# Layer-norm statistics of two tiles in one VectorE instruction, and x + beta divided between GpSimd and VectorE

## The chip, the cores and the metric

The kernel runs on one core of one Trainium2 chip. The metric is the device time of one execution in microseconds. Three runs of the kernel before gave 680.88, 681.93 and 682.16 us; the median is 681.93 us.

## The reference

One layer of a graph network with 50000 nodes of 128 features, 25000 edges sorted by their target, 32 features per edge and one number (coordination) per node, all in f32:

```python
h = maximum(layernorm(x), 0)                       # no gamma, beta
e = concat(h[src], h[dst], edge_attr, c[src], c[dst])
messages = silu(e @ mW1 + mb1) @ mW2 + mb2
aggregated = segment_sum(messages, dst)            # per node
u = silu(concat(h, aggregated, c) @ uW1 + ub1) @ uW2 + ub2
out = x + layernorm(h + u) * gamma + beta
```

So there are three layer norms: of the rows gathered for an edge's two ends, of each node's own row, and of the update h + u. Each needs the mean and the variance of 128 numbers per row.

## The kernel before, in words

Work goes in steps. An edge step takes 512 edges: 4 tiles of 128 edges for each of two ends, gathered from HBM by eight indirect DMAs which GpSimd issues (L452). A node step takes 1024 nodes, 8 tiles of 128 nodes. Both kinds have 49 steps. Iteration n of the pipeline works on edge step n and, four behind it (NODE_LAG), on node step n - 4, with further stages of neighbouring steps in the same iteration. Each engine runs its own program, and semaphores tie them. `PIPELINES` says which iterations stand in the hardware loop of four iterations (9 to 44 before); those ahead and behind are unrolled, and 54 is the last.

VectorE's iteration, in its order (function `body` from L858, `k` is the node step of the iteration, `prev` and `done` the two before it, `later` and `ahead` the node steps two and four further, `new` the edge step):

- `y_stat` and `finish` for each of 8 tiles in turn: statistics of the update of `prev` (L935, read from PSUM), and the output of `done`, centred * rstd + x_beta (L902);
- `sum_means` (L944, y_sum), then `match_nodes(0)` (L888, builds the 0/1 matrix by which TensorE sums messages into nodes), `halve_means` (L951, y_mean), `match_nodes(1)`;
- `centre` for 8 tiles (L872): (update - mean) * gamma, which frees the PSUM tile ps_upd for TensorE;
- statistics of the 8 gathered tiles of `new` (L986, L987), after their gathers have landed;
- the chain from statistics to rstd and -mean * rstd: s_sub, s_add, s_m2, s_sq, var, guess, root_a, root_e, root_p, root_q, root_r, rstd, minus (L1004 to L1039), on 24 columns, one per tile. The statistics of x for `ahead` (L925) stand between them as fillers. ScalarE normalises with the result.

A `bn_stats` instruction gives six numbers per partition: count, mean and sum of squared deviations of the elements at even places, and the same three for the odd places. On one tile of 128 features the two halves have to be joined, which is what y_sum, y_mean, s_sub, s_add, s_m2, s_sq and var do.

x + beta (x_beta) is read by `finish` two iterations after it is made. GpSimd makes it for a whole node step in one instruction (L475), after its eight gathers and after both matches of the iteration (`match_ready`); for the first two node steps VectorE does (L916). GpSimd also loads gamma, beta and iota rows (`load_rows`, L488 to L493), between the gathers of edge step 0 and those of step 1. x itself is loaded by ScalarE's queue (L672), the message windows by SyncE's, eight loads per step (L393), which must follow the storing of the messages (L367).

TensorE's iteration: first layer of the edges (L531, L532, L535), turning of coordinates and x_norm (L543, L553), second layer (L563, L565), node products with `match` (L605, L608), turning of ends_norm (L576), update (L620, L622).

Of the kernel before, what the change touches and what calls it, by code (L numbers as in the profile page):

```python
# [6 lines left out]
P = 128  # L7
H = 128
# [3 lines left out]
EPS = 1e-5  # L12
# [123 lines left out]
PIPELINES = {WHOLE: (9, 45, NODE_STEPS + NODE_LAG + 2),  # L136
# [16 lines left out]
def gnn_layer(nc, rows, x_steps, ends, dst_all, dst_seen, attr, node_vec, mW1, mb1, mW2, mb2, uW1, ub1, uW2, ub2,  # L153
# [17 lines left out]
    with ctx:  # L171
# [55 lines left out]
        stats = sb("stats", [P, NS, 6])  # L227
        s_add, s_sub, s_m2, s_sq, var = (sb(n, [P, NS]) for n in ("s_add", "s_sub", "s_m2", "s_sq", "var"))
        y_sum, y_mean = sb("y_sum", [P, N_TILES]), sb("y_mean", [P, N_TILES])
# [42 lines left out]
        x_beta_ready, x_norm_ready = sem("x_beta_ready"), sem("x_norm_ready")  # L272
# [4 lines left out]
        y_mean_ready, half_out = sem("y_mean_ready"), sem("half_out")  # L277
# [34 lines left out]
        def _(sp):  # L312
# [125 lines left out]
            sp.dma_start(msgs[EDGES_PAD:MSG_ROWS, :], zeros[:, 0:2, :].rearrange("p a b -> p (a b)")[:, 0:MSG_ROW]).then_inc(tail_cleared, 16)  # L438
            sp.wait_ge(first_ready, 1)
# [8 lines left out]
        def _(pool):  # L448
# [8 lines left out]
            def body(it):  # L457
# [30 lines left out]
            def load_rows():  # L488
                for dst, source in (
                        (gamma_row[:, 0, :], gamma.rearrange("(o n) -> o n", o=1).broadcast_to([P, H])),  # L490
                        (beta_row[:, 0, :], beta.rearrange("(o n) -> o n", o=1).broadcast_to([P, H]))):
                    pool.dma_start(dst, source).then_inc(late_loaded, 16)
                pool.dma_start(iota[:, :, :].rearrange("p j m -> p (j m)"), iota_row.rearrange("(o n) -> o n", o=1).broadcast_to([P, N_STEP])).then_inc(iota_loaded, 16)  # L493

            run_steps(pool, body, scatter, load_rows)
# [139 lines left out]
        def _(act):  # L635
# [25 lines left out]
            def body(it):  # L661
# [4 lines left out]
                def load_nodes():  # L666
# [4 lines left out]
                    act.wait_ge(x_beta_ready, further.n - RING + 1)  # L671
                    act.dma_start(x_in[further.slot][:, :, :], x_v[further.n]).then_inc(x_loaded[further.slot], 16)  # L672
# [116 lines left out]
        STAT_OPS = 10  # L789
# [6 lines left out]
        def _(dve):  # L796
# [61 lines left out]
            def body(it):  # L858
                new = it.edge(0)
                ahead, nxt, later, k, prev, done = it.node(4), it.node(3), it.node(2), it.node(0), it.node(-1), it.node(-2)  # L860
                b, was = it.phase % RING, (it.phase - 1) % RING

                def centre(j):
# [3 lines left out]
                    if j == 0:  # L867
                        dve.wait_ge(y_mean_ready, 2 * prev.n + 2)
# [3 lines left out]
                    last = V.scalar_tensor_tensor(centred[:, j, :], ps_upd[:, j * P:(j + 1) * P], y_mean[:, j:j + 1], gamma_row[:, 0, :],  # L872
# [20 lines left out]
                def finish(j):  # L893
# [3 lines left out]
                    if j == 0:  # L897
                        dve.wait_ge(centred_ready, 2 * done.n + 2)
                        dve.wait_ge(rstd_ready, 2 * it.stats_before())
                        dve.wait_ge(x_beta_ready, done.n + 1)  # L900
                        wait(dve, stored[done.half], 16 * done.fills2)
# [7 lines left out]
                def add_beta():  # L909

                    if not later or k:
                        return
                    wait(dve, out_ready, later.n - RING + 1)
                    if isinstance(later.n, int) and later.n == 0:
                        dve.wait_ge(late_loaded, 16 * N_LATE)
                    V.tensor_tensor(x_beta[later.slot][:, :, :], x_in[later.slot][:, :, :],  # L916
# [196 lines left out]
```

## Time and profile before

| | |
|---|---|
| median of three runs | 681.93 us |
| the profiled execution: time | 680.75 us |
| its span, first to last instruction | 678.9 us |
| granted TensorE clock, mean | 0.986 of full |
| TensorE busy | 623.9 us (92%) |
| VectorE busy | 618.1 us (91%) |
| ScalarE busy | 545.7 us (80%) |
| GpSimd busy | 496.5 us (73%), of it 382.4 in 392 gathers and 111.3 in 47 x_beta |
| largest waits | GpSimd's gathers, issue, 106.4; ScalarE's hidden_n for TensorE 57.1; VectorE for gathers 23.6; TensorE for match 16.7 |

GpSimd's issue gaps, some 0.3 us ahead of each gather, belong to issuing a gather, so its load is its busy time and these. Three engines are busy for nine tenths of the span or close to it once that is counted, so shares of busy time don't tell which one sets the pace; the rows of one step, in order of time, do. Instructions on VectorE overlap: one starts before the last has ended, so the distance between starts, not the duration, is what an instruction costs there.

### The profile page before, as it was taken

To read this page: it belongs to the slowest core of one execution; us is meant where nothing else is said; L and a number is where in the kernel's file an instruction comes from. 1 tells how busy PE (TensorE), PEld (TensorE's weight loads), DVE (VectorE), ACT (ScalarE), POOL (GpSimd) and SP (SyncE) were. 2 spreads that over 40 slices of the span, in tenths; PEclk is the share of its full clock that TensorE was granted. 3 is DMA by queue.
4 is the path that set the end of the run, shared out by engine and by line. 5 is a ranking of instruction groups with operands and counts; after the bars stand their busy time and mean duration, and the time that the engine had idled before them with its cause. 6 is when DMAs were issued, how large, how long until landed. Compare 5 with 4: busy or idle time off the path is not lost.

```text
span 678.9 us, 17136 instructions
## 1 busy us (share of the span) xinstructions
PE 623.9 (92%) x3764; PEld 449.7 (66%) x3764; DVE 618.1 (91%) x2905; ACT 545.7 (80%) x1181; POOL 496.5 (73%) x447
## 2 busy tenths in 40 slices
PE   2889999999999999999999999999999999999982
PEld 1346787676676676676676676676676676776662
DVE  4747999999999999999999999999999999999887
ACT  1468999888888888888888888888888888899720
POOL 7778887887787787887787887887787788874200
PEclk9988999999999999999999999999999999999987
DMA  4645476677677677577677577676677677674422
GB/s 109 219 119 136 138 215 195 166 206 194 164 199 199 164 199 199 166 201 195 164 207 191 164 202 195 165 200 197 164 200 198 162 198 202 179 218 119 130 80 98
DMA packets 91986, 119.05 MB, mean 175 GB/s; under 512 B 20250, under 2 KB 65493, under 8 KB 91944
## 3 DMA queue, kind: packets, MB, share of 16 engines
q1 hardware_dynamic: 64436, 43.37, 23.9%
q0 software_dynamic: 12752, 26.57, 20.3%
q10 hardware_dynamic: 14756, 48.66, 19.0%
q8 instruction: 13, 0.21, 0.1%
q14 instruction: 29, 0.24, 0.1%
HBM read 79.63 MB, written 38.70 MB: 174 GB/s over the span
## 4 chain that ended last, share of the span: by engine, by line
POOL 27%; DVE 27%; issue 24%; PE 9%; DMA 8%; ACT 2%; SPq 1%; DVEq 1%; POOLq 0%; ACTq 0%
POOL ends_in L452 27%; DVE y_out L902 7%; DMA ends_in<-in_rows,end_idx 6%; DVE stats L935 5%; DVE stats L925 3%; DVE centred L872 3%; DVE stats L987 2%; DVE stats L986 2%; SPq L393 1%; PE ps_hid L608 1%; PE ps_upd L620 1%; ACT ends_norm L682 1%; PE ps_t L576 1%; PE ps_e L565 1%; PE ps_hid L605 1%
## 5 line engine op out<-in xcount | busy, mean ns | idle before, releaser
L452 POOL DMA_INDIRECT ends_in<-in_rows,end_idx x392 | 382.4, 975 | 114.8 <-issue 106.4
L682 ACT ACTIVATE ends_norm<-ends_in,minus,rstd 128x128 f32<-128x128 f32 x392 | 160.3, 482 | 5.9 <-DVE minus L1039 5.5
L682 ACT ACTIVATE x_norm<-x_in,minus,rstd 128x128 f32<-128x128 f32 x392 | 155.5, 481 | 0.0
L608 PEld LDWEIGHTS ps_hid<-match,msg_in 113*128 113x128 f32 x784 | 99.6, 191 | 78.5 <-DVE match L888 48.8
L475 POOL TENSOR_TENSOR x_beta<-x_in,beta_row 128x1024 f32<-128x1024 f32 x47 | 111.3, 2367 | 30.7 <-DVE y_out L902 18.5
L902 DVE SCALAR_TENSOR_TENSOR y_out<-centred,rstd,x_beta 128x128 f32<-128x128 f32 x392 | 128.1, 336 | 2.7 <-issue 0.4
L608 PE MATMUL ps_hid<-match,msg_in 113*128 113x128 f32 x784 | 107.6, 280 | 17.5 <-DVE match L888 16.7
L935 DVE BATCH_NORM_STATS2 stats<-ps_upd 128x6 f32<-128x128 f32 x392 | 109.8, 289 | 4.5 <-issue 4.0
L780 ACT ACTIVATE hidden_n<-ps_hid,node_bias 128x512 f32<-128x512 f32 x98 | 67.0, 683 | 58.0 <-PE ps_hid L608 57.1
L620 PE MATMUL ps_upd<-w_out,hidden_n 128*128 128x128 f32 x784 | 104.7, 277 | 5.2 <-DVE centred L872 5.2
L872 DVE SCALAR_TENSOR_TENSOR centred<-ps_upd,y_mean,gamma_row 128x128 f32<-128x128 f32 x392 | 107.3, 338 | 0.0
L925 DVE BATCH_NORM_STATS2 stats<-x_in 128x6 f32<-128x128 f32 x392 | 100.7, 283 | 0.7
L605 PE MATMUL ps_hid<-h_t,w_node 128*128 128x512 f32 x196 | 100.7, 595 | 0.0
L620 PEld LDWEIGHTS ps_upd<-w_out,hidden_n 128*128 128x128 f32 x784 | 96.2, 193 | 5.8 <-DVE centred L872 5.8
L888 DVE SCALAR_TENSOR_TENSOR match<-iota_sb,const_sb,msg_in 112x512 f32<-112x512 f32 x98 | 73.2, 752 | 8.1 <-DMA msg_in<-msgs 6.7
L986 DVE BATCH_NORM_STATS2 stats<-ends_in 128x6 f32<-128x128 f32 x196 | 54.7, 279 | 24.3 <-DMA ends_in<-in_rows,end_idx 23.6
L706 ACT ACTIVATE h_t<-ps_t,b_col 128x1024 f32<-128x1024 f32 x49 | 54.5, 1113 | 16.1 <-PE ps_t L553 15.2
L742 ACT ACTIVATE ends_t<-ps_t 128x1024 f32<-128x1024 f32 x49 | 50.2, 1024 | 12.5 <-PE ps_t L576 12.5
L622 PE MATMUL ps_upd<-const_sb,h_t 128*128 128x128 f32 x392 | 59.4, 275 | 0.0
L576 PE MATMUL ps_t<-const_sb,ends_norm 128*128 128x128 f32 x392 | 51.9, 276 | 4.2 <-ACT ends_norm L682 4.2
L535 PE MATMUL ps_e<-feat_t,w_feat 34*128 34x512 f32 x98 | 55.0, 642 | 0.0
L987 DVE BATCH_NORM_STATS2 stats<-ends_in 128x6 f32<-128x128 f32 x196 | 54.0, 275 | 0.0
(92 smaller groups left out, 787.6 us busy)
## 6 DMA issues: line engine op xcount, KB each, us to landing
out<-y_out ACTq DMA_DIRECT2D x48, 512.0 KB, 2.9
x_in<-in_x_steps ACTq DMA_DIRECT2D x44, 512.0 KB
msg_in<-msgs SPq DMA_DIRECT2D x392, 56.4 KB
msgs<-msg SPq DMA_DIRECT2D x49, 258.0 KB, 2.5
ends_in<-in_rows,end_idx POOLq DMA_INDIRECT x392
feat_t<-in_attr SPq DMA_DIRECT2D x25, 128.0 KB
x_in<-in_x_steps SPq DMA_DIRECT2D x5, 512.0 KB
feat_t<-coords SPq DMA_DIRECT2D x98, 2.0 KB
```

The lines of the kernel that those rows point to most:

```text
L452: nc.gpsimd.indirect_dma_start(out=dst, out_offset=None, in_=rows, in_offset=bass.IndirectOffsetOnAxis(ap=end_idx[s.slot // 2][:, s.slot % ...
L475: nc.gpsimd.tensor_tensor(x_beta[later.slot][:, :, :], x_in[later.slot][:, :, :], beta_row[:, :, :].broadcast_to([P, N_TILES, H]), ALU.add ...
L605: nc.tensor.matmul(ps_hid[:, bank], w_node[:, :], h_t[k.half][:, bank], start=True, stop=False)
L608: last = nc.tensor.matmul(ps_hid[:, cols(j)], msg_in[k.half][0:WINDOW + 1, j, 0:H], match[k.half][0:WINDOW + 1, j, :], start=False, stop=j ...
L620: nc.tensor.matmul(ps_upd[:, cols(j)], hidden_n[:, cols(j)], w_out[:, :], start=j == tiles[0], stop=False)
L682: return nc.scalar.activation(dst, source, function, bias=minus[was][:, c:c + 1], scale=rstd[was][:, c:c + 1])
L872: last = V.scalar_tensor_tensor(centred[:, j, :], ps_upd[:, j * P:(j + 1) * P], y_mean[:, j:j + 1], gamma_row[:, 0, :], ALU.subtract, ALU. ...
L888: V.scalar_tensor_tensor(match[k.half][0:WINDOW, tiles, :], iota[0:WINDOW, tiles, :], const[0:WINDOW, bass.ds(C_BASE + N_TILES * k.n, 1)], ...
L902: last = V.scalar_tensor_tensor(y_out[done.half][:, j, :], centred[:, j, :], rstd[was][:, Y_AT + j:Y_AT + j + 1], x_beta[done.slot][:, j, ...
L925: last = V.bn_stats(stats[:, X_AT + j, :], x_in[n.slot][:, j, :])
L935: last = V.bn_stats(stats[:, Y_AT + j, :], ps_upd[:, j * P:(j + 1) * P])
L986: V.bn_stats(stats[:, t, :], ends_in[new.slot][:, 0, t, 0:H])
```

## The change

- `bn_stats` reads two neighbouring tiles at once, with the view `p t f -> p f t`: element 0 of the first tile, element 0 of the second, element 1 of the first, and so on. The even places are then the first tile and the odd ones the second, so the six numbers are count, mean and squared deviations of each. y_sum, y_mean, s_sub, s_add, s_m2 and s_sq go; `var` is one operation on the stored squares, `centre` and `minus` read the mean from the statistics. A step has 12 statistics instructions on 256 elements instead of 24 on 128. The fillers in the chain are four pairs. The statistics have two buffers now, since those of `ahead` are written while the iteration's own are read.
- x_beta: GpSimd makes the first four tiles of a node step (semaphore x_beta_head), VectorE the last four, at the end of its iteration behind `minus`. The first two node steps stay whole on VectorE.
- SyncE issues the loads of gamma, beta and iota, near its start, ahead of its wait for first_ready.
- The hardware loop covers iterations 11 to 46 instead of 9 to 44.

```diff
-PIPELINES = {WHOLE: (9, 45, NODE_STEPS + NODE_LAG + 2),
+PIPELINES = {WHOLE: (11, 47, NODE_STEPS + NODE_LAG + 2),
...
-        stats = sb("stats", [P, NS, 6])
+        stats = [sb(f"stats{b}", [P, NS, 3]) for b in range(2)]
...
+            for dst, source in (
+                    (gamma_row[:, 0, :], gamma.rearrange("(o n) -> o n", o=1).broadcast_to([P, H])),
+                    (beta_row[:, 0, :], beta.rearrange("(o n) -> o n", o=1).broadcast_to([P, H]))):
+                sp.dma_start(dst, source).then_inc(late_loaded, 16)
+            sp.dma_start(iota[:, :, :].rearrange("p j m -> p (j m)"), iota_row.rearrange("(o n) -> o n", o=1).broadcast_to([P, N_STEP])).then_inc(iota_loaded, 16)
             sp.wait_ge(first_ready, 1)
...
-                    if isinstance(later.n, int) and later.n == 2:
-                        pool.wait_ge(x_beta_ready, 2)
-                    else:
-                        wait(pool, match_ready, 2 * later.n - 2)
-                    nc.gpsimd.tensor_tensor(x_beta[later.slot][:, :, :], x_in[later.slot][:, :, :],
-                                            beta_row[:, :, :].broadcast_to([P, N_TILES, H]), ALU.add).then_inc(x_beta_ready, 1)
+                    wait(pool, match_ready, 2 * later.n - 2)
+                    nc.gpsimd.tensor_tensor(x_beta[later.slot][:, 0:N_TILES // 2, :], x_in[later.slot][:, 0:N_TILES // 2, :],
+                                            beta_row[:, :, :].broadcast_to([P, N_TILES // 2, H]), ALU.add).then_inc(x_beta_head, 1)
...
+                def pair_stats(into, c, tiles):
+
+                    return V.bn_stats(into[:, c:c + 2, :].rearrange("p c s -> p (c s)"), tiles.rearrange("p t f -> p f t"))
...
-                    if not later or k:
-                        return
+                    if not later:
+                        return
+                    if k:
+                        dve.wait_ge(x_loaded[later.slot], 16 * (later.fills4 + 1))
                     wait(dve, out_ready, later.n - RING + 1)
...
+                    tiles = slice(HALF if k else 0, N_TILES)
+                    V.tensor_tensor(x_beta[later.slot][:, tiles, :], x_in[later.slot][:, tiles, :],
+                                    beta_row[:, :, :].broadcast_to([P, tiles.stop - tiles.start, H]), ALU.add).then_inc(x_beta_ready, 1)
...
-                V.tensor_tensor(s_sub[:, at], stats[:, at, 1], stats[:, at, 4], ALU.subtract).then_inc(stat_ops, 1)
-                V.tensor_tensor(s_add[:, at], stats[:, at, 1], stats[:, at, 4], ALU.add)
                 if late:
-                    halve_means()
-                V.scalar_tensor_tensor(s_m2[:, at], stats[:, at, 2], H * EPS, stats[:, at, 5], ALU.add, ALU.add).then_inc(stat_ops, 1)
+                    dve.wait_ge(y_stats, prev.n + 1)
+                V.tensor_scalar(var[:, at], own_stats[:, at, SQUARES], 1.0 / H, EPS, ALU.mult, ALU.add).then_inc(stat_ops, 1)
+                between(0)
                 dve.wait_ge(stat_ops, base + 1)
-                V.scalar_tensor_tensor(s_sq[:, at], s_sub[:, at], 0.25, s_sub[:, at], ALU.mult, ALU.mult).then_inc(stat_ops, 1)
-                dve.wait_ge(stat_ops, base + 2)
-                between(0)
-                dve.wait_ge(stat_ops, base + 3)
-                V.scalar_tensor_tensor(var[:, at], s_m2[:, at], 1.0 / H, s_sq[:, at], ALU.mult, ALU.add).then_inc(stat_ops, 1)
-                between(1)
...
-                V.scalar_tensor_tensor(minus[b][:, at], s_add[:, at], -0.5, rstd[b][:, at], ALU.mult, ALU.mult).then_inc(rstd_ready, 1)
+                V.scalar_tensor_tensor(minus[b][:, at], own_stats[:, at, MEAN], -1.0, rstd[b][:, at], ALU.mult, ALU.mult).then_inc(rstd_ready, 1)
+                if k:
+                    add_beta()
```

## Rows read from the trace of the kernel before

**Rows 1.** Stretches, all engines: length, busy us (instructions) of each engine, clock, DMA.
```profile
65.84:113.85 48.01, 48.01 (x306) 36.06 (x305) 44.23 (x207) 44.24 (x98) 38.97 (x34) 1.00 0.63 186
...
267.00:369.00 102.00, 98.18 (x611) 71.42 (x610) 97.69 (x459) 88.88 (x194) 80.41 (x73) 1.00 0.68 187
...
572.73:622.25 49.52, 49.07 (x307) 35.73 (x305) 48.41 (x230) 44.36 (x98) 37.76 (x34) 1.00 0.66 193
...
634.25:678.90 44.65, 26.88 (x165) 21.02 (x163) 36.13 (x170) 12.33 (x23) 2.35 (x1) 0.86 0.28 92
```

**Rows 2.** Time order, TensorE, first edge product: start us, us, engine, line.
```profile
65.84 1.02 PE L531 MATMUL ps_e<-ends_t,w_src 128*128 128x512 f32 x2
...
113.85 1.02 PE L531 MATMUL ps_e<-ends_t,w_src 128*128 128x512 f32 x2
...
634.25 1.02 PE L531 MATMUL ps_e<-ends_t,w_src 128*128 128x512 f32 x2
```

**Rows 3.** Time order, VectorE, one step and the next one's end.
```profile
301.80 0.29 DVE L986 BATCH_NORM_STATS2 stats<-ends_in 128x6 f32<-128x128 f32 x1 [0.38 <-DMA ends_in<-in_rows,end_idx]
...
303.49 0.20 DVE L1004 TENSOR_TENSOR s_sub<-stats 128x24 f32<-128x24 f32 x1
...
306.51 0.18 DVE L1039 SCALAR_TENSOR_TENSOR minus<-s_add,rstd 128x24 f32<-128x24 f32 x1
...
310.51 0.16 DVE L944 TENSOR_TENSOR y_sum<-stats 128x8 f32<-128x8 f32 x1
310.71 0.80 DVE L888 SCALAR_TENSOR_TENSOR match<-iota_sb,const_sb,msg_in 112x512 f32<-112x512 f32 x1
311.43 0.29 DVE L951 TENSOR_SCALAR y_mean<-y_sum 128x8 f32<-128x8 f32 x1
311.51 0.74 DVE L888 SCALAR_TENSOR_TENSOR match<-iota_sb,const_sb,msg_in 112x512 f32<-112x512 f32 x1
...
314.24 0.28 DVE L986 BATCH_NORM_STATS2 stats<-ends_in 128x6 f32<-128x128 f32 x1
...
327.35 0.29 DVE L986 BATCH_NORM_STATS2 stats<-ends_in 128x6 f32<-128x128 f32 x1
```

**Rows 4.** Time order, GpSimd, the same step.
```profile
312.33 2.36 POOL L475 TENSOR_TENSOR x_beta<-x_in,beta_row 128x1024 f32<-128x1024 f32 x1 [0.59 <-DVE match L888]
...
314.84 0.96 POOL L452 DMA_INDIRECT ends_in<-in_rows,end_idx  x1 [0.16 <-issue]
...
323.76 0.95 POOL L452 DMA_INDIRECT ends_in<-in_rows,end_idx  x1 [0.30 <-DVE y_out L902]
```

**Rows 5.** Time order, VectorE, late node step: eight statistics without other work between.
```profile
651.13 1.67 DVE L935 BATCH_NORM_STATS2 stats<-ps_upd 128x6 f32<-128x128 f32 x8
```

**Rows 6.** Groups by shape, VectorE: busy us, mean ns, idle before.
```profile
L1004 DVE TENSOR_TENSOR s_sub<-stats 128x24 f32<-128x24 f32 x44 | 9.2, 209 | 1.5
...
L1010 DVE SCALAR_TENSOR_TENSOR s_sq<-s_sub 128x24 f32<-128x24 f32 x44 | 7.6, 174 | 0.0
...
L1004 DVE TENSOR_TENSOR s_sub<-stats 128x8 f32<-128x8 f32 x5 | 0.8, 166 | 0.0
...
L1010 DVE SCALAR_TENSOR_TENSOR s_sq<-s_sub 128x8 f32<-128x8 f32 x5 | 0.8, 159 | 0.0
```

**Rows 7.** The whole x + beta on VectorE (groups, time order), a gather beside it.
```profile
L916 DVE TENSOR_TENSOR x_beta<-x_in,beta_row 128x1024 f32<-128x1024 f32 x2 | 2.4, 1218 | 0.0
...
41.85 1.22 DVE L916 TENSOR_TENSOR x_beta<-x_in,beta_row 128x1024 f32<-128x1024 f32 x1
...
42.47 1.42 POOL L452 DMA_INDIRECT ends_in<-in_rows,end_idx  x1 [0.30 <-issue]
```

**Rows 8.** Time order, start: GpSimd's queue, then VectorE's wait for step 1.
```profile
14.16 0.60 POOL L492 DMA_DIRECT2D gamma_row<-in_gamma  x1
...
16.16 1.01 POOL L452 DMA_INDIRECT ends_in<-in_rows,end_idx  x1 [0.30 <-issue]
...
27.92 0.29 DVE L986 BATCH_NORM_STATS2 stats<-ends_in 128x6 f32<-128x128 f32 x1 [3.63 <-DMA ends_in<-in_rows,end_idx]
```

More of the change, by code:

```diff
@@ L226, in gnn_layer @@
         NS = 3 * N_TILES
-        stats = sb("stats", [P, NS, 6])
-        s_add, s_sub, s_m2, s_sq, var = (sb(n, [P, NS]) for n in ("s_add", "s_sub", "s_m2", "s_sq", "var"))
-        y_sum, y_mean = sb("y_sum", [P, N_TILES]), sb("y_mean", [P, N_TILES])
+        stats = [sb(f"stats{b}", [P, NS, 3]) for b in range(2)]
+        var = sb("var", [P, NS])
         guess, root_a, root_e, root_p, root_q, root_r = (
@@ L486, in scatter @@
                     ).then_inc(lone_scattered, 16)
[L488 to L495, printed above, removed]
+            run_steps(pool, body, scatter)
         @block.tensor
@@ L671, in load_nodes @@
                     act.wait_ge(x_beta_ready, further.n - RING + 1)
+                    wait(act, x_beta_head, further.n - RING - 1)
                     act.dma_start(x_in[further.slot][:, :, :], x_v[further.n]).then_inc(x_loaded[further.slot], 16)
@@ L871, in centre @@
                             dve.wait_ge(late_loaded, 16 * N_LATE)
-                    last = V.scalar_tensor_tensor(centred[:, j, :], ps_upd[:, j * P:(j + 1) * P], y_mean[:, j:j + 1], gamma_row[:, 0, :],
+                    last = V.scalar_tensor_tensor(centred[:, j, :], ps_upd[:, j * P:(j + 1) * P], own_stats[:, Y_AT + j, MEAN:MEAN + 1], gamma_row[:, 0, :],
                                                   ALU.subtract, ALU.mult)
@@ L900, in finish @@
                         dve.wait_ge(x_beta_ready, done.n + 1)
+                        wait(dve, x_beta_head, done.n - 1)
                         wait(dve, stored[done.half], 16 * done.fills2)
@@ L958, in between @@
                         centre(j)
+                        centre(j + 1)
                     elif k:
-                        x_stat(ahead, j)
+                        x_stat(ahead, j, next_stats)
                 if late:
@@ L966, in body @@
                         finish(j)
-                    for j in range(N_TILES):
+                    for j in range(0, N_TILES, 2):
                         y_stat(j)
-                    sum_means()
                 else:
-                    for j in range(N_TILES):
+                    for j in range(0, N_TILES, 2):
                         y_stat(j)
                         finish(j)
-                    sum_means()
+                        finish(j + 1)
                     match_nodes(0)
-                    halve_means()
                     match_nodes(1)
@@ L980, in body @@
                 if nxt and it.begins_nodes():
-                    for j in range(N_TILES):
-                        x_stat(nxt, j)
+                    for j in range(0, N_TILES, 2):
+                        x_stat(nxt, j, own_stats)
                 if new:
                     dve.wait_ge(gathered[new.slot], (new.fills4 + 1) * 32 * E_TILES)
-                    for t in range(E_TILES):
-                        V.bn_stats(stats[:, t, :], ends_in[new.slot][:, 0, t, 0:H])
-                        last = V.bn_stats(stats[:, E_TILES + t, :], ends_in[new.slot][:, 1, t, 0:H])
+                    for c in range(0, 2 * E_TILES, 2):
+                        side, t = divmod(c, E_TILES)
+                        last = pair_stats(own_stats, c, ends_in[new.slot][:, side, t:t + 2, 0:H])
                     last.then_inc(ends_stats, 1)
                 if not (new or nxt or prev):
-                    for j in range(N_TILES):
-                        x_stat(ahead, j)
+                    for j in range(0, N_TILES, 2):
+                        x_stat(ahead, j, next_stats)
                     add_beta()
@@ L1038, in body @@
                 dve.wait_ge(rstd_ready, 2 * it.stats_before() + 1)
-                V.scalar_tensor_tensor(minus[b][:, at], s_add[:, at], -0.5, rstd[b][:, at], ALU.mult, ALU.mult).then_inc(rstd_ready, 1)
+                V.scalar_tensor_tensor(minus[b][:, at], own_stats[:, at, MEAN], -1.0, rstd[b][:, at], ALU.mult, ALU.mult).then_inc(rstd_ready, 1)
+                if k:
+                    add_beta()
                 if not (k or late):
-                    for j in range(N_TILES):
-                        x_stat(ahead, j)
+                    for j in range(0, N_TILES, 2):
+                        x_stat(ahead, j, next_stats)
             def scatter():
```

48 lines of the change are left out of this document (17 added, 31 removed).

## The prediction

> **What bounds the kernel now.** I read four views in this order: the granted clock and busy time by stretches, the matmul rows of TensorE, one step of VectorE in order of time, and GpSimd's rows of the same step. The reader should see three cycles of nearly the same length, only one of which is a floor that the change leaves alone.
>
> TensorE first. From 65.84 to 113.85 us TensorE is busy in all 48.01 of 48.01 us at a granted clock of 1.00, that is at 2.4 GHz [rows 1]. In that stretch its first edge product (L531) starts four times at exactly (113.85 - 65.84) / 4 = 12.00 us apart [rows 2]. So 12.00 us is what one step of products costs if nothing is late. From 113.85 to 634.25 the same product starts 41 more times, one every 520.4 / 41 = 12.69 us [rows 2], with TensorE busy in only 98.18 of 102.00 us [rows 1]. ScalarE, at 44.24 / 4 = 11.06 us per step in the fast stretch [rows 1], isn't the bound. Over the 45 steps from 65.84 to 634.25 the time above the floor is 568.4 - 45 x 12.00 = 28.4 us. That is what is to be had in the steady part.
>
> VectorE next. It starts one step's edge statistics at 301.80 and the next at 314.24, and between the two it never waits for long: 12.44 us of its own work [rows 3]. It is a bound above 12.00. The first steps got by with 12.00 because VectorE could fall behind its lead there for a while.
>
> GpSimd last. Its turn is eight gathers, 314.84 to 323.76 + 0.95 = 324.71, so 9.87 us, and x + beta, which starts at 312.33 and holds the next gather until 314.84, so 2.51 us [rows 4]: 12.38 us. The two engines are also tied in a ring that takes two steps: edge statistics at 301.80, second match done at 311.51 + 0.74 = 312.25 (10.45 us), x + beta, eight gathers to 324.71, data landed and the statistics of the step after next at 327.35, 2.64 us later [rows 3, 4]. That is 25.55 us for two steps, 12.78 each, which is close to the 12.69 seen. So the ring decides, VectorE's own turn comes next, then GpSimd's, and TensorE has 0.69 us of air in each step.
>
> **The change part by part.**
>
> *Two tiles per statistics instruction.* Eight of them on 128 columns take 1.67 us with 0.29 for the last, so one starts every (1.67 - 0.29) / 7 = 0.197 us [rows 5]. An element costs about (1218 - 174) / 1000 = 1.05 ns, from the 1024-column add and a 24-column operation [rows 6, 7], so 128 of them are 0.134 us and 0.063 us of each start is fixed. A pair has one fixed part less. If an element costs the same in it, a pair takes 0.331 instead of 0.394 us. A step has 24 tiles of statistics (8 for edges, 8 of x, 8 of the update), 12 pairs: 12 x 0.063 = 0.76 us less on VectorE per step.
>
> The unshown cost is the order in which a pair reads: element by element it jumps between two tiles 128 words apart. Low end: nothing extra (it can't be below, since still 256 elements are read at the rate of a dense stream). High end from the nearest rows: the operation that reads two sources with a step of six words grows from 166 to 209 ns between 8 and 24 columns, 2.69 ns per element, where the dense one grows from 159 to 174, 0.94 ns [rows 6]. The surplus of 1.75 ns, shared by its two jumping sources, is 0.87 ns per source; on 12 x 256 elements it would be 2.7 us per step. I take the low end: the rows that jump have two input streams, and a statistics instruction has one and writes six words in all, so I hold it nearer to the dense single stream. This is the choice that I trust least.
>
> The Trainium skill speaks to this twice. "Vector Engine (DVE) Microarchitecture Reference", Measured stream behaviour on trn2, says that a port keeps its rate only for pairs of adjacent words, and that a jump at each element costs some 0.65 cycle; by that rule the twelve pairs would take an estimated 2.1 us per step more and the change would lose. The same section says that a one-source operation alternating between two regions, writing one word per two read, kept the full rate, which would be this case. No statistics row here reads in that order, so the trace leaves it open; the six-word rows agree that jumping can cost.
>
> *Small operations.* The sum and half of the means go: y_sum at 310.51 holds the match until 310.71 (0.20 us), y_mean at 311.43 holds the second until 311.51 (0.08) [rows 3]. Of the chain from statistics to rstd five operations (s_sub, s_add, s_m2, s_sq, var) become one. The chain from s_sub at 303.49 to minus at 306.51 is 3.02 us; without eight statistics at 0.197 it is 1.44 us for twelve starts, 0.12 each [rows 3, 5], so four fewer are 0.48 us. Some of it comes back, since four fillers stand where eight did and root_r now waits openly for root_p; I count 0.12 for that, bounded by 0 and by 0.36 (three more starts' worth). Together 0.64 us less.
>
> *x + beta.* GpSimd's half: between 2.36 / 2 = 1.18 us less (cost by size) and nothing less; I take 1.18, since 1024 columns at 2.3 ns each leave little that is fixed [rows 4]. VectorE's half is new: 512 x 1.05 ns + 0.063 = 0.60 us [rows 6, 7], at the end of its step, behind minus. Queued behind it are only the next step's update statistics, then finish and match; ScalarE has its rstd already. Its waits (x loaded, out_ready of the finish done earlier in the same step) are over by then.
>
> It has a price on the other engine too. When VectorE adds x + beta for a whole step at 41.85, the gather at 42.47 takes 1.42 us, against 0.95 for others [rows 4, 7]: 0.47 us more. For half the size, between nothing (it falls between gathers) and 0.47; I take 0.2 per step.
>
> *Sum per step.* VectorE: 12.44 - 0.76 - 0.64 + 0.60 = 11.64 us. GpSimd: 12.38 - 1.18 + 0.2 = 11.40. The ring of two steps passes VectorE's work, x + beta and the gathers once: 25.55 - 0.80 - 1.18 + 0.20 = 23.77, 11.89 per step. All three fall under TensorE's 12.00, which is late next. The ring's air is only 0.11 us, and a late landing or the loop's branch eats it now and then, so I take 12.05 with 12.00 as floor and, with all of the unkind ends but the jumping (0.24 for the small operations, 0.27 for the gather, 1.18 for x + beta), (23.77 + 1.69) / 2 = 12.73 as ceiling. 45 x 12.05 = 542.3, against 568.4: -26.1 us.
>
> *Rows by SyncE.* The three loads at 14.16 to 16.16 leave GpSimd's queue between the first eight gathers and the next [rows 8]; gathers follow 0.30 us after one another elsewhere, so 2.0 - 0.3 = 1.7 us. The ramp hangs on those gathers: VectorE waits for step 1's until 27.92 [rows 8] and the chain of waits runs back through them. SyncE issues the three ahead of its wait for first_ready, a wait that is done only after 10 us, and nothing else is queued there; TensorE's match and VectorE's gamma are needed tens of microseconds later. -1.7 us, between 0 and -2.0.
>
> *Tail.* From 634.25 to 678.90 [rows 1] TensorE is busy for 26.88 of 44.65 us and VectorE works off the last nodes. Three rounds there have four pairs less fixed cost (0.25) and no y_sum (0.20): -1.4 us, between 0 and -2.
>
> *Loops from step 11.* Steps 9 and 10 are unrolled, 45 and 46 looped. The unrolled steps from 572.73 to 622.25 took 49.52 / 4 = 12.38 each, all 41 together 12.69 [rows 1, 2]; two for two, so nothing.
>
> The profiled execution took 680.75 us, of which 678.9 are its span. 680.75 - 26.1 - 1.7 - 1.4 = 651.6. The median of the runs, 681.93, lies 1.2 above the profiled one, so the forecast is 653 us.
>
> **The rivals.**
>
> *A pair costs as much as two* (jumping costs 0.25 ns per element, or only the pairs that read PSUM pay, or a fixed part per pair grows). Then 0.76 us per step isn't saved: VectorE 12.40, ring (23.77 + 0.76) / 2 = 12.27, a step some 12.42: 45 x 0.27 = 12.2 us saved, tail 0.6, ramp 1.7: 667. The same place is reached if the ring keeps more than I think. For it: 0.11 us of air. Against it: the four steps at 12.00 show that the message loads and ScalarE keep up.
>
> *Jumping costs in full* (the other side). Place: every pair on VectorE. Price: between 0.44 and 0.87 ns per element, the middle 0.65 x 3072 = 2.0 us per step, VectorE 13.64. It loses from the point where VectorE's turn passes 12.69, that is (12.69 - 11.64) / 3072 = 0.34 ns per element. 45 x 13.64 = 613.8, +45.4, ramp -1.7, tail about 0: 725 us; at the bounds 695 and 755. For it: the six-word rows [rows 6]. Against: their two sources.
>
> *Nothing that can be told*: half-costs and savings meet, about 681. It needs a jump of almost exactly 0.34 ns.
>
> **How the numbers follow.** Forecast case, 647 to 660: 0.60. Pair as two, 660 to 679: 0.17. Nothing: 0.03. Slower: 0.20. A measurement of this kernel can tell about 0.2% from no change. Faster is the first two, 0.77. The range leaves out the slower case: 647 (45 x 12.00, and 2 more from ramp and tail) less one for the runs' spread gives 646; upwards to 680. Within it 0.79.
>
> **What would show it.** Pairs starting every 0.33 us, on x, edges and PSUM alike, with L531 at 12.00 to 12.1 apart, show the first step right; pairs at 0.50 show the slow rival. x + beta near 1.2 us on GpSimd and 0.60 on VectorE, waits of TensorE for match nearly gone, VectorE idle some 0.3 us per step and a gather now and then over 1.1 us show the rest. The second batch of gathers should start near 14.4. I am wrong if VectorE stays busy throughout and steps stay above 12.4.

## The result and the profile after

The changed kernel takes 648.99 us (median of 4 runs, 648.67 to 649.35), against 681.62 us for the kernel before beside it: a ratio of 0.9519, 95% interval 0.9503 to 0.9535. Ratios here and below are estimated from the executions in the faster of the two states alone, so they differ a little from quotients of the medians. The forecast was 653 us. The profiled execution took 648.95 us, its span is 647.1 us.

| | before | after | difference |
|---|---|---|---|
| start of the edge product of iteration 5 | 65.84 | 61.97 | -3.87 |
| 45 steps from there | 568.41 | 542.45 | -25.96 |
| rest of the span | 44.65 | 42.68 | -1.97 |
| VectorE busy, us | 618.1 | 573.5 | -44.6 |
| GpSimd busy, us | 496.5 | 455.1 | -41.4 |
| TensorE busy | 92% | 94% | |

The stretches of the changed kernel (columns as in [rows 1]):

```profile
65.00:113.00 48.00, 47.79 (x302) 36.05 (x305) 44.27 (x158) 44.25 (x97) 37.11 (x37) 1.00 0.63 185
...
113.00:300.00 187.00, 185.65 (x1169) 140.31 (x1184) 174.93 (x615) 170.40 (x371) 143.68 (x140) 1.00 0.68 198
...
300.00:500.00 200.00, 198.57 (x1240) 148.07 (x1255) 188.66 (x669) 181.82 (x400) 156.39 (x151) 1.00 0.69 198
...
605.00:647.10 42.10, 26.16 (x162) 20.74 (x161) 32.59 (x130) 11.75 (x21) 1.27 (x1) 0.86 0.29 96
```

TensorE is busy for 198.57 of 200 us in the middle, where before it was 98.18 of 102 [rows 1]. The first edge product of a step, in time order (it is line 525 now), against [rows 2]:

```profile
61.97 1.02 PE L525 MATMUL ps_e<-ends_t,w_src 128*128 128x512 f32 x2
...
109.97 0.59 PE L525 MATMUL ps_e<-ends_t,w_src 128*128 128x512 f32 x1
...
326.78 1.02 PE L525 MATMUL ps_e<-ends_t,w_src 128*128 128x512 f32 x2
...
339.58 1.02 PE L525 MATMUL ps_e<-ends_t,w_src 128*128 128x512 f32 x2
...
604.42 1.02 PE L525 MATMUL ps_e<-ends_t,w_src 128*128 128x512 f32 x2
```

The distances tell the steps: (109.97 - 61.97) / 4 = 12.00, and over all 45 of them (604.42 - 61.97) / 45 = 12.054 us. 39 of them are 12.00 to within 0.01. One slow one, of 12.78, starts at 193.99; the others stand together: 12.80 from 326.78, then 12.09, 12.32, 12.19, and 12.21 at 400. The first of them in its rows:

```profile
186.84 1.88 POOL L456 DMA_INDIRECT ends_in<-in_rows,end_idx  x1 [0.30 <-DVE y_out L904]
...
191.75 1.43 DVE L862 BATCH_NORM_STATS2 stats<-ends_in 128x6 f32<-128x256 f32 x4 [1.77 <-DMA ends_in<-in_rows,end_idx]
...
200.48 0.71 PE L602 MATMUL ps_hid<-match,msg_in 113*128 113x128 f32 x4 [0.51 <-DVE match L889]
```

The last gather of a step takes 1.88 us, VectorE waits 1.77 us for what it brings, and TensorE in its turn 0.51 us for the match. In such a step the prediction's ring decides.

VectorE's step in time order, the counterpart of [rows 3]; L862 is the pair's statistics, L921 the half of x + beta, L904 finish:

```profile
303.52 0.68 DVE L921 TENSOR_TENSOR x_beta<-x_in,beta_row 128x512 f32<-128x512 f32 x1
304.13 0.42 DVE L862 BATCH_NORM_STATS2 stats<-ps_upd 128x6 f32<-128x256 f32 x1
304.47 0.60 DVE L904 SCALAR_TENSOR_TENSOR y_out<-centred,rstd,x_beta 128x128 f32<-128x128 f32 x2
...
307.56 1.40 DVE L889 SCALAR_TENSOR_TENSOR match<-iota_sb,const_sb,msg_in 112x512 f32<-112x512 f32 x2
308.88 2.15 DVE L873 SCALAR_TENSOR_TENSOR centred<-ps_upd,stats,gamma_row 128x128 f32<-128x128 f32 x8
311.12 1.43 DVE L862 BATCH_NORM_STATS2 stats<-ends_in 128x6 f32<-128x256 f32 x4
312.59 0.18 DVE L996 TENSOR_SCALAR var<-stats 128x24 f32<-128x24 f32 x1
312.68 0.43 DVE L862 BATCH_NORM_STATS2 stats<-x_in 128x6 f32<-128x256 f32 x1
313.02 0.16 DVE L999 TENSOR_SCALAR guess<-var 128x24 int32<-128x24 int32 x1
...
315.19 0.68 DVE L921 TENSOR_TENSOR x_beta<-x_in,beta_row 128x512 f32<-128x512 f32 x1
...
324.45 1.43 DVE L862 BATCH_NORM_STATS2 stats<-ends_in 128x6 f32<-128x256 f32 x4 [1.77 <-DMA ends_in<-in_rows,end_idx]
```

From one x + beta at 303.52 to the next at 315.19 it is 11.67 us, without a wait of more than 0.2 us. A pair holds the next instruction for 304.47 - 304.13 = 0.34 us. In the following step VectorE waits 1.77 us for gathers: it isn't the bound. Over the 17 steps between 100 and 580 us in which it waits no longer than that either, its turn is 11.58 us on average. GpSimd's rows beside that step:

```profile
302.38 0.95 POOL L456 DMA_INDIRECT ends_in<-in_rows,end_idx  x1 [0.30 <-issue]
...
303.63 1.39 POOL L456 DMA_INDIRECT ends_in<-in_rows,end_idx  x1 [0.30 <-issue]
...
307.90 1.22 POOL L456 DMA_INDIRECT ends_in<-in_rows,end_idx  x1 [0.30 <-DVE y_out L904]
...
309.13 1.28 POOL L476 TENSOR_TENSOR x_beta<-x_in,beta_row 128x512 f32<-128x512 f32 x1
```

x + beta on half the tiles takes 1.28 us where the whole took 2.36 [rows 4]. Two of these gathers are long, 1.39 us beside VectorE's x + beta at 303.52 and 1.22 beside its match at 307.56.

The start, the counterpart of [rows 8]:

```profile
12.63 0.94 POOL L456 DMA_INDIRECT ends_in<-in_rows,end_idx  x1 [0.30 <-issue]
...
13.88 0.94 POOL L456 DMA_INDIRECT ends_in<-in_rows,end_idx  x1 [0.30 <-issue]
...
25.18 1.43 DVE L862 BATCH_NORM_STATS2 stats<-ends_in 128x6 f32<-128x256 f32 x4 [2.03 <-DMA ends_in<-in_rows,end_idx]
```

The second batch of gathers follows at once, at 13.88 instead of 16.16. Of these 2.28 us the rows are worth 1.70; the last gather of the first batch starts 0.58 us earlier by itself (12.63, in the kernel before 13.21). Step 1's statistics start at 25.18 instead of 27.92.

### The profile page after: what moved, and what is told of

Its sections match the earlier page's. It is cut to its first block, busy times and chain, and to the rows that moved or that the text cites. A ratio compares the mean times of both kernels' runs of the same rounds, so it can differ in the third digit from the quotient of the medians.

```text
span 647.1 us, 16188 instructions
## 1 busy us (share of the span) xinstructions
PE 610.1 (94%) x3716; PEld 451.7 (70%) x3764; DVE 573.5 (89%) x2050; ACT 541.9 (84%) x1181; POOL 455.1 (70%) x444
## 4 chain that ended last, share of the span: by engine, by line
PE 69%; DVE 12%; DMA 6%; issue 5%; POOL 3%; ACT 2%; SPq 1%; DVEq 0%; POOLq 0%; ACTq 0%
PE ps_hid L602 10%; PE ps_upd L614 10%; PE ps_hid L599 9%; PE ps_e L559 6%; PE ps_e L529 6%; PE ps_t L547 5%; PE ps_t L570 5%; PE ps_e L525 5%; PE ps_e L526 5%; PE ps_upd L616 5%; DMA ends_in<-in_rows,end_idx 4%; DVE stats L862 4%; DVE y_out L904 3%; POOL ends_in L456 3%; DVE centred L873 1%
## 5 line engine op out<-in xcount | busy, mean ns | idle before, releaser
L456 POOL DMA_INDIRECT ends_in<-in_rows,end_idx x392 | 393.8, 1005 | 117.5 <-issue 105.3
L904 DVE SCALAR_TENSOR_TENSOR y_out<-centred,rstd,x_beta 128x128 f32<-128x128 f32 x392 | 115.6, 338 | 0.4
L873 DVE SCALAR_TENSOR_TENSOR centred<-ps_upd,stats,gamma_row 128x128 f32<-128x128 f32 x392 | 106.5, 339 | 0.0
L602 PE MATMUL ps_hid<-match,msg_in 113*128 113x128 f32 x784 | 104.0, 275 | 1.1 <-DVE match L889 1.0
L862 DVE BATCH_NORM_STATS2 stats<-ends_in 128x6 f32<-128x256 f32 x196 | 69.8, 418 | 32.3 <-DMA ends_in<-in_rows,end_idx 32.2
L476 POOL TENSOR_TENSOR x_beta<-x_in,beta_row 128x512 f32<-128x512 f32 x47 | 60.1, 1279 | 38.2 <-DVE y_out L904 20.7
L862 DVE BATCH_NORM_STATS2 stats<-x_in 128x6 f32<-128x256 f32 x196 | 81.8, 427 | 0.5 <-issue 0.5
L862 DVE BATCH_NORM_STATS2 stats<-ps_upd 128x6 f32<-128x256 f32 x196 | 81.1, 421 | 0.0
L559 PE MATMUL ps_e<-w_fold,hidden_e 128*128 128x128 f32 x392 | 52.3, 277 | 3.6 <-ACT hidden_e L685 1.2
L547 PE MATMUL ps_t<-const_sb,x_norm 128*128 128x128 f32 x392 | 51.7, 276 | 2.8 <-ACT x_norm L677 2.5
```

Of the source, the lines that this page charges most:

```text
L456: nc.gpsimd.indirect_dma_start(out=dst, out_offset=None, in_=rows, in_offset=bass.IndirectOffsetOnAxis(ap=end_idx[s.slot // 2][:, s.slot % ...
L547: last = nc.tensor.transpose(ps_t[:, cols(j)], x_norm[near.half][:, j, :], ident)
L559: last = nc.tensor.matmul(ps_e[:, cols(t)], hidden_e[:, cols(t)], w_fold[:, :], start=False, stop=t == E_TILES - 1)
L602: last = nc.tensor.matmul(ps_hid[:, cols(j)], msg_in[k.half][0:WINDOW + 1, j, 0:H], match[k.half][0:WINDOW + 1, j, :], start=False, stop=j ...
L862: return V.bn_stats(into[:, c:c + 2, :].rearrange("p c s -> p (c s)"), tiles.rearrange("p t f -> p f t"))
L904: last = V.scalar_tensor_tensor(y_out[done.half][:, j, :], centred[:, j, :], rstd[was][:, Y_AT + j:Y_AT + j + 1], x_beta[done.slot][:, j, ...
```

## The experiments

Two theories stood against each other. The first is the prediction's: three cycles of 12.4 to 12.8 us per step (VectorE, GpSimd, and the ring through both) lay over TensorE's 12.00, so the parts of the change give their full gain only together. The rival: VectorE alone set the pace and the pairs did all of it, the rest being trimmings. Besides it was open what a pair's jumping read costs, what the rows at the start bring, and what binds now. Unless said otherwise a ratio is to the kernel before, on the same chip.

**Pairs alone.** The kernel before with the first bullet of the change:

```diff
-        stats = sb("stats", [P, NS, 6])
+        stats = [sb(f"stats{b}", [P, NS, 3]) for b in range(2)]
...
+                    return V.bn_stats(into[:, c:c + 2, :].rearrange("p c s -> p (c s)"), tiles.rearrange("p t f -> p f t"))
```

> The kernel before with the pair statistics and the shorter chain alone; x + beta whole on GpSimd, rows by GpSimd, loop from step 9. Theory (three cycles, GpSimd's own turn 12.38 us is the next one above TensorE's 12.00): VectorE's turn falls from 12.44 to about 11.1, the ring to (25.55 - 1.3) / 2 = 12.1, and GpSimd's 12.4 decides: steps of 12.4, 45 x 0.23 = 10 us less and 1.5 in the tail, 670 us. Rival (VectorE alone set the pace): steps of 12.0, 652 us.

686.18 us, ratio 1.0039 (1.0019 to 1.0059): no gain, a slight loss, though VectorE's busy time fell from 618.1 to 548.5 us. Both expectations missed, the rival's by 34 us and mine by 16. GpSimd in time order:

```profile
303.31 2.37 POOL L474 TENSOR_TENSOR x_beta<-x_in,beta_row 128x1024 f32<-128x1024 f32 x1
...
313.51 1.88 POOL L451 DMA_INDIRECT ends_in<-in_rows,end_idx  x1 [0.30 <-DVE y_out L907]
...
316.65 2.37 POOL L474 TENSOR_TENSOR x_beta<-x_in,beta_row 128x1024 f32<-128x1024 f32 x1
...
329.83 2.37 POOL L474 TENSOR_TENSOR x_beta<-x_in,beta_row 128x1024 f32<-128x1024 f32 x1
```

Its turn is 13.34 and then 13.18 us, not 12.38. One of its gathers takes 1.88 us. VectorE at that time:

```profile
313.18 1.40 DVE L893 SCALAR_TENSOR_TENSOR match<-iota_sb,const_sb,msg_in 112x512 f32<-112x512 f32 x2
...
319.63 1.44 DVE L866 BATCH_NORM_STATS2 stats<-ends_in 128x6 f32<-128x256 f32 x4 [2.99 <-DMA ends_in<-in_rows,end_idx]
```

The gather at 313.51 runs beside the two matches (1.40 us, two SBUF inputs each), and VectorE waits 2.99 us later on for what the gathers bring. Over the gathers issued between 100 and 600 us, read one by one in time order, those that start while a match runs take 1.55 us on average (39 of them) and those that start beside a statistics instruction 0.946 (136). In the kernel before the 34 that start beside a match averaged 1.00 and took at most 1.40. What a gather pays goes by when it starts within VectorE's sequence. In the kernel before, the gather at 310.79, 0.08 us after the first match of [rows 3], takes 0.94:

```profile
310.79 0.94 POOL L452 DMA_INDIRECT ends_in<-in_rows,end_idx  x1 [0.30 <-DVE y_out L902]
```

In pairs_alone those that start 0.08 or 0.09 us after the first match take 2.14 to 2.15 (six of them; this is one, its match starts at 222.15, so it ends 0.83 us after the second match does):

```profile
222.24 2.14 POOL L451 DMA_INDIRECT ends_in<-in_rows,end_idx  x1 [0.30 <-issue]
```

Two things differ: y_mean stands between the two matches in the kernel before and they follow back to back in the other, and what ran ahead of the gather. Which of them lets the gather through wasn't tried. The mean of all gathers is 1.035 us where it was 0.972 in the kernel before, so GpSimd's turn grows by 8 x 0.063 = 0.50 us, and 12.38 + 0.50 = 12.88 is what the 45 steps average, where 12.4 was expected. That GpSimd decides is seen in its waits too: between 100 and 600 us it never waits more than 0.05 us, apart from the 0.3 ahead of each gather, and its 38 turns there average 12.96 us.

**Half alone.** The kernel before with x + beta divided, else untouched:

```diff
+                    tiles = slice(HALF if k else 0, N_TILES)
...
-                add_beta()
+                if not k:
+                    add_beta()
...
+                if k:
+                    add_beta()
```

> The kernel before with x + beta divided alone. Theory: VectorE's turn grows by 0.60 to 13.04 us and decides though GpSimd's falls to 11.3: steps of 13.0 to 13.1, 45 x 0.4 = 18 us more, 700 us. Rival (GpSimd sets the pace before, VectorE only follows it): the ring falls to (25.55 + 0.60 - 1.18) / 2 = 12.5, steps of 12.5, about 675 us.

690.29 us, ratio 1.0111 (1.0091 to 1.0131). Slower, as the theory wants and the rival doesn't. The 45 steps average 12.84 us; in the loop they lie between 12.8 and 13.2. VectorE decides: 36 of its 38 turns between 100 and 600 us are without a wait. GpSimd now waits for the match instead (from the list of waits: total us, times, longest):

```profile
POOL x_beta L472 <- DVE match L886: 65.4, 41, 1.8
```

It was 10.8 us in 17 waits before. The theory's 13.04 was too high by 0.1 in the loop, and I had let the four steps of 12.00 at the start, and 12.64 at the end, count as slow.

**Whole x + beta on GpSimd, the rest of the change kept.**

```diff
-                    nc.gpsimd.tensor_tensor(x_beta[later.slot][:, 0:N_TILES // 2, :], x_in[later.slot][:, 0:N_TILES // 2, :],
+                    nc.gpsimd.tensor_tensor(x_beta[later.slot][:, :, :], x_in[later.slot][:, :, :],
...
-                    if not later:
+                    if not later or k:
```

> The changed kernel with x + beta put back whole on GpSimd, all else as changed. Theory after pairs_alone: GpSimd's turn decides, and it's longer than the 12.4 us worked out, since gathers that run beside VectorE's match take up to 1.9 us: steps alternate between 12.0 and 14, about 12.85 on average as in pairs_alone; with the shorter ramp 683 us. Rival (the time of pairs_alone came from rows or loop, which it left as before): 12.4 us per step, 665 us.

684.91 us, ratio 1.0036 (1.0012 to 1.0060); 12.71 us per step in the profiled execution, which with 678.17 us was the shortest of its ten. So the time of pairs_alone doesn't come from rows or loop: without the division of x + beta the pairs bring nothing, with rows and loop or without.

**Dense read.** The changed kernel, with a pair read tile after tile; the statistics then belong to no single tile:

```diff
-                    return V.bn_stats(into[:, c:c + 2, :].rearrange("p c s -> p (c s)"), tiles.rearrange("p t f -> p f t"))
+                    return V.bn_stats(into[:, c:c + 2, :].rearrange("p c s -> p (c s)"), tiles)
```

> The changed kernel with each pair read tile after tile instead of alternating, so the statistics belong to no single tile; the output's norms are left wrong by that, the work is the same. If jumping between the two tiles costs nothing: a pair starts every 0.34 us as before and the time is 649.0 us within 0.3%. If jumping costs anything hidden in the 0.34, a pair falls to 0.33 or less and VectorE's busy time by some us, the time hardly, as TensorE decides.

649.64 us, ratio 0.9496 (0.9471 to 0.9521), the changed kernel's 0.9519 within it. Groups by shape, first of the dense kernel:

```profile
L862 DVE BATCH_NORM_STATS2 stats<-x_in 128x6 f32<-128x256 f32 x196 | 80.7, 419 | 0.6 <-issue 0.6
```

and of the changed one, with all three kinds of pair:

```profile
L862 DVE BATCH_NORM_STATS2 stats<-x_in 128x6 f32<-128x256 f32 x196 | 81.8, 427 | 0.5 <-issue 0.5
...
L862 DVE BATCH_NORM_STATS2 stats<-ps_upd 128x6 f32<-128x256 f32 x196 | 81.1, 421 | 0.0
...
L862 DVE BATCH_NORM_STATS2 stats<-ends_in 128x6 f32<-128x256 f32 x196 | 69.8, 418 | 32.3 <-DMA ends_in<-in_rows,end_idx 32.2
```

419 ns against 427 for x: 8 ns on 256 elements, 0.03 ns per element, where the forecast's high end was 0.87. PSUM reads no slower (421 ns). From start to start it is 0.34 us in both. Jumping between two tiles costs this one-source statistics instruction nothing that counts.

**Lighter TensorE.** The changed kernel without the transposes that add h to the update; the output lacks that term:

```diff
-                    for j in tiles:
-                        last = nc.tensor.matmul(ps_upd[:, cols(j)], h_t[k.half][:, cols(j)], ident, is_transpose=True,
-                                                start=False, stop=j == tiles[-1])
```

> The changed kernel without the transposes of h that TensorE adds to the update (16 short products less per step, about 0.88 us), so the update lacks the + h. Theory (TensorE sets the pace now, VectorE's turn of 11.65 us and GpSimd's of about 11.9 are next): steps fall from 12.05 to 11.9 only, 45 x 0.15 = 7 us less, 642 us. Rival 1 (TensorE has far more air behind it): 11.2, 610 us. Rival 2 (TensorE isn't the bound): 649 us.

645.25 us, ratio 0.9438 (0.9404 to 0.9473), that is 0.8% under the changed kernel's ratio: some 5.5 us, near the theory's 7 and far from both rivals. (The transposes left out are eight per step, not sixteen; the 0.88 us agrees with the starts around them in the kernel before.) Edge products in time order, and the stretch 180 to 560:

```profile
72.70 1.02 PE L525 MATMUL ps_e<-ends_t,w_src 128*128 128x512 f32 x2
...
84.37 1.02 PE L525 MATMUL ps_e<-ends_t,w_src 128*128 128x512 f32 x2
...
180.00:560.00 380.00, 361.52 (x2143) 252.71 (x2142) 359.66 (x1271) 343.80 (x762) 299.33 (x286) 1.00 0.70 198
```

and the same stretch of the changed kernel:

```profile
180.00:560.00 380.00, 377.27 (x2358) 282.37 (x2388) 358.27 (x1267) 345.98 (x759) 294.22 (x286) 1.00 0.69 198
```

The shortest step is 84.37 - 72.70 = 11.67 us now (TensorE then waits a little for ScalarE's hidden_e, 18.9 us in 46 waits, so it isn't 11.1), but the 45 average 11.975. TensorE's idle time in the stretch grew from 2.7 to 18.5 us of 380. Its weight loads wait 31.8 us for the match, 9.6 in the changed kernel. Giving TensorE 0.33 us or more brought 0.08 per step. So TensorE is the bound in the changed kernel, and the ring through VectorE and GpSimd lies right behind it, at 11.9 to 12.0.

**Rows by SyncE alone**, on the kernel before:

```diff
+                sp.dma_start(dst, source).then_inc(late_loaded, 16)
...
-            run_steps(pool, body, scatter, load_rows)
+            run_steps(pool, body, scatter)
```

> The kernel before with gamma, beta and iota loaded by SyncE alone. Theory as predicted: the second batch of gathers starts 1.7 us earlier and the whole ramp with it, 680 us, steps unchanged at 12.7. Second theory, from the trace of after, where the ramp is 3.9 us shorter: the earlier gathers also shorten TensorE's wait enough that its clock stays at 2.4 GHz between 30 and 40 us, so 677.8 us. Rival (the load is a buffer that VectorE's slower steps eat up again before the end): no change.

682.06 us, ratio 0.9981 (0.9968 to 0.9994): -1.3 us, between -0.4 and -2.2. The first theory's 1.7 us lies in that interval. The second theory's 4 us falls, though the granted clock was 1.00 between 30 and 40 us as it wanted, and the rival's "no change" falls narrowly. In the profiled execution the edge product of iteration 5 starts at 64.30 instead of 65.84, the slower cycles catch TensorE one step earlier, and its last edge product starts at 635.48, 1.2 us later than before. Whether the slower cycles eat a part of the gain can't be told from one execution of each.

**Rows by GpSimd and loop from 9, the rest of the change kept.**

```diff
-PIPELINES = {WHOLE: (11, 47, NODE_STEPS + NODE_LAG + 2),
+PIPELINES = {WHOLE: (9, 45, NODE_STEPS + NODE_LAG + 2),
...
-            run_steps(pool, body, scatter)
+            run_steps(pool, body, scatter, load_rows)
```

> The changed kernel with gamma, beta and iota loaded by GpSimd again and the loop over 9 to 44 again, so the two main parts stand alone. Theory: no engine eats the ramp's gain up here, so its loss shows in full, 1.7 to 3.9 us by the start of the fifth iteration's edge product (about 64 to 66 us instead of 62), and the loop's place does nothing to the steps: 651 to 653 where the changed kernel has 649. Rival: as in rows_alone, 1.3 us or less, 650.

650.69 us, ratio 0.9524 (0.9500 to 0.9548), just under the theory's 651 and near the rival's 650. The profiled execution is the longest of its six, 653.52 us. In it the edge product of iteration 5 starts at 65.26, the 45 steps average 12.07, as in the changed kernel. The two main parts alone give the steady gain. The small ones together are worth 1.7 us by the medians, which two different chips gave, and by the ratios anything between nothing and 2 us. The stretch 30 to 40 us, and VectorE's wait for step 1, of this kernel:

```profile
30.00:40.00 10.00, 6.87 (x19) 3.29 (x17) 3.96 (x17) 7.76 (x18) 7.56 (x9) 0.83 0.39 94
...
27.76 1.43 DVE L864 BATCH_NORM_STATS2 stats<-ends_in 128x6 f32<-128x256 f32 x4 [4.15 <-DMA ends_in<-in_rows,end_idx]
```

two stretches of the kernel before:

```profile
30.00:40.00 10.00, 6.91 (x21) 3.61 (x20) 4.65 (x26) 6.52 (x16) 7.56 (x9) 0.83 0.42 94
50.00:60.00 10.00, 8.52 (x36) 5.37 (x34) 8.00 (x36) 8.14 (x19) 8.20 (x8) 0.83 0.38 88
```

and the same two of the changed kernel:

```profile
30.00:40.00 10.00, 8.23 (x31) 3.88 (x31) 3.72 (x13) 7.59 (x18) 7.72 (x8) 1.00 0.38 95
50.00:60.00 10.00, 8.45 (x51) 7.40 (x53) 6.25 (x20) 8.35 (x19) 8.21 (x8) 0.83 0.36 92
```

Where the granted clock is 0.83 on average, a part of the stretch ran at 1.2 GHz instead of 2.4. Between 30 and 40 us this happened in the kernel before and in this one, after TensorE had waited 3.09 and 3.13 us for the second step's ends; pairs_alone and half_alone, which have the rows on GpSimd as well, waited 2.52 and 2.76 us and show 1.00, as do all six with the rows on SyncE. Between 50 and 60 us it happened in six of the ten profiled executions, with rows on either engine. So the ramps have to be compared at a like number of such falls. With none between 50 and 60, the edge product of iteration 5 starts at 64.06 us with the rows on GpSimd (pairs_alone) and at 62.01 and 61.40 with them on SyncE. With one fall, there alone, it starts at 64.79 (half_alone) against 61.97, 64.30 and 63.65, 63.3 on average. The rows are thus worth some 1.5 to 2.4 us, by few executions that differ in more than the rows, and the 3.87 seen holds a second fall of the clock that the changed kernel's execution lacked.

**Rows alone put back, and the loop alone put back.** These two ran only on a chip on which the kernel before itself took 1016 us, with a mean granted clock of 0.85 in the two profiles, so nothing is concluded from them (1006.73 and 1019.83 us). Two kernels above ran there as well, the whole x + beta on GpSimd with 1017.34 and the lighter TensorE with 1010.45 us; their numbers above are from other chips.

> The changed kernel with gamma, beta and iota loaded by GpSimd again. Theory: here no engine eats the ramp's gain up, so its loss shows in full, 1.7 to 3.9 us: 650.7 to 652.9. Rival: as small as in rows_alone, 1.3 us or less.

> The changed kernel with the hardware loop over iterations 9 to 44. Theory: two iterations for two, no change beyond 0.2%: 649 us. Rival: the steps that leave the loop late (45 and 46) lose by it, or those that enter it early, 0.3 to 0.5 us per turn: up to 1.5 us either way.

What the loop's place is worth by itself stays open; rows_loop_back bounds it to what is left beside the ramp, under 2 us.

**Three tiles on GpSimd, five on VectorE.**

```diff
-                    nc.gpsimd.tensor_tensor(x_beta[later.slot][:, 0:N_TILES // 2, :], x_in[later.slot][:, 0:N_TILES // 2, :],
+                    nc.gpsimd.tensor_tensor(x_beta[later.slot][:, 0:3, :], x_in[later.slot][:, 0:3, :],
...
-                    tiles = slice(HALF if k else 0, N_TILES)
+                    tiles = slice(3 if k else 0, N_TILES)
```

> The changed kernel with three tiles of x + beta on GpSimd and five on VectorE. Theory (GpSimd's turn and the ring, lengthened by gathers beside match, make the few steps above 12.00; VectorE at 11.65 has 0.35 to give): 0.27 us less on GpSimd, 0.13 more on VectorE, the slow steps thin out, 45 x 12.02: 647.5 us, 0.2% less than the changed kernel. Rival (VectorE's longer add meets more gathers and its turn has no air): 651 us.

647.74 us, ratio 0.9488 (0.9466 to 0.9510), the lowest of all that compute the whole layer. Against the changed kernel's 0.9519 the intervals touch, so it is probably but not surely faster. Its steps average 12.03 us; all are 12.00 to within 0.01 but three, 12.71 at 181.42, 12.42 at 470.18 and 12.08 at 482.60. The stretch 180 to 560:

```profile
180.00:560.00 380.00, 377.72 (x2364) 283.60 (x2395) 363.01 (x1272) 346.76 (x760) 290.59 (x286) 1.00 0.69 198
```

TensorE is busy for 377.72 us of 380 (377.27 in the changed kernel), so this is the end of what dividing x + beta can bring: (12.054 - 12.00) x 45 = 2.4 us were left.

## Why the prediction was right, point by point

The forecast of 653 us was 4 us above the measured 649, and its mechanism held: three cycles lay above 12.00 us, all three were brought under it on average, and TensorE's floor is what is left. The account of GpSimd within it was right in its sum and wrong in one of its terms.

*The floor.* 12.00 us per step, read from four steps of [rows 2], was reached and not passed; 12.05 was taken, 12.054 came. That all engines kept up with 12.00 for four steps of the trace before was the best evidence there was: it showed that message loads and ScalarE could follow. lighter_tensor_2 shows that it is TensorE's.

*Pairs.* 0.331 us per pair forecast, 0.34 measured; the choice of the low end for jumping, least trusted, is right by dense_read. The Trainium skill, "Vector Engine (DVE) Microarchitecture Reference", Measured stream behaviour on trn2, gives a cost of some 0.65 cycle for a jump at each element and, for a one-source operation that alternates between two regions, the full rate; the 419 and 427 ns here agree with the second and not with the first.

*Small operations.* The chain from var to minus is 315.08 - 312.59 = 2.49 us, without its four pairs of 0.34 it is 1.13 where it was 1.44: 0.31 less, 0.36 was forecast.

*VectorE's sum.* 11.64 forecast, 11.67 measured, 11.58 on average. x + beta there 0.60, measured 304.13 - 303.52 = 0.61.

*GpSimd and the ring.* x + beta came to 1.28 instead of 1.18 us, which puts 2367 - 1279 = 1.09 us on 512 columns and 0.19 on what is fixed. The stretching of gathers was mis-sized in kind rather than in sum: I priced VectorE's x + beta at 0.2 us per step and nothing for match, which in [rows 3, 4] let its gathers pass. In the changed kernel the mean gather grew from 0.972 to 1.007 us, 0.28 per step, with 1.35 for those that start beside match (31 gathers) and 1.12 for those beside x + beta (19). GpSimd's turn without its waits is 11.60 us on average between 100 and 580 us, where 11.40 was forecast, but single turns reach 12.7. The sum came out near by luck of the phase; in pairs_alone the same effect was 0.5 us more per step than before and took the whole gain. The ring's air of 0.11 us, called too little to trust, is what the slow steps at 194 and around 330 to 410 us spent. The range had a slip as well: its ceiling of 12.73 put the unkind ends into the ring alone, and with the same ends GpSimd's own turn was 12.38 + 0.47 = 12.85.

*Rows by SyncE.* 1.7 us forecast, and 1.70 is what leaves GpSimd's queue; the second batch started 2.28 us earlier, step 1's statistics 2.7, and the ramp was 3.9 shorter. The missing terms are the 0.58 us that the first batch was ahead by itself and the clock: [rows 1] and its neighbours were read from 65.84 on, and its falls in the ramp weren't looked at, two in the profiled execution of before and one in that of after. The forecast for the profiled execution was 651.6 us and 648.95 came; of the 2.65 us between, 2.2 are this part and 0.6 the tail.

*Tail.* 1.4 forecast, 1.97 came. Not tried apart.

*Loop.* Nothing forecast; under 2 us either way is all that is shown.

*Rivals.* "A pair costs as much as two" fell with the 0.34 us from start to start, where two single statistics take 0.39, and "jumping costs in full" with dense_read. What neither of them nor the forecast held, and what experiments brought out, is that either main part by itself makes the kernel slower: 1.0039 and 1.0111, and 0.9524 together.

## What to carry to other kernels

Where two or three engines' turns are of nearly equal length, work out each turn and the ring through them, since a part that shortens only one of them can bring nothing or a loss, and the gain appears when all are under the next floor. Look for a stretch of the trace in which the next engine already ran unhindered: its step there is the time that can be reached. An engine made faster also changes how its instructions stand to another's, so price contention for every place where they could meet, not only as they meet in the trace.

## What the runs showed of the hardware

A gather issued by GpSimd takes 0.94 to 0.95 us in peace. What it takes beside a VectorE instruction with two SBUF inputs goes by when it starts. Two rows of the changed kernel beside x + beta on VectorE:

```profile
352.89 0.68 DVE L921 TENSOR_TENSOR x_beta<-x_in,beta_row 128x512 f32<-128x512 f32 x1
...
353.32 1.07 POOL L456 DMA_INDIRECT ends_in<-in_rows,end_idx  x1 [0.30 <-issue]
```

This gather ends at 354.39, 0.82 us after the add ends at 353.57. So do those at 303.63 and 315.29, which start 0.1 us after the add and take 1.39 and 1.40. All 18 gathers of the changed kernel between 100 and 600 us that start 0.1 to 0.53 us after the add end 0.81 to 0.82 us after it, and all 31 of three_on_gpsimd, whose add is 0.82 us long, that start 0.04 to 0.45 us after it. Those that start up to 0.6 us before the add take 0.94 to 0.95 in both kernels, and so do those of the changed kernel that start 0.59 us or more after its start. In half_alone none starts in between, and all of its 49 gathers that run beside the add are in peace. A gather thus pays by its place in VectorE's sequence, and not by how much of it overlaps.

Beside VectorE's two matches back to back (0.75 us each, two SBUF inputs) a gather takes 1.55 us on average and up to 2.15 in pairs_alone, and 1.35 on average and up to 1.88 in the changed kernel, while with y_mean between them most gathers of the kernel before passed in 0.94 to 1.08. Those that start beside `finish`, which has two SBUF tensor inputs too but is 0.34 us long, take 0.99 to 1.02 on average. Statistics of 256 elements that alternate between two tiles cost 418 to 427 ns from SBUF and 421 from PSUM, within 8 ns of the dense read.
